# A recommendation tower on one core: row numbers added in one Pool instruction, 416 embedding gathers written out in a row

## What is computed

```python
e = jnp.stack([tbl_0[ids[:, 0]], ..., tbl_25[ids[:, 25]]], axis=1)      # 2048 x 26 x 64
x = layer_norm(dense_t @ Wd.T, gd, bd)                                 # 2048 x 128
y = layer_norm(jnp.einsum('bnd,ed->bne', e, Ws), gs, bs)               # 64 -> 128 for each row
y = layer_norm(jnp.einsum('bne,pn->bep', y, Wsi), gsi, bsi)            # 26 features -> 32
T = jnp.concatenate([x[:, None, :], jnp.swapaxes(y, 1, 2)], axis=1)    # 33 vectors of 128
Z = jnp.einsum('bnd,bmd->bnm', T, T)                                   # their products
out = layer_norm(Z[:, TRIL_I, TRIL_J] @ Wl.T, gl, bl)                  # 384 of 512 are used
h = concatenate([out, dense]); relu layers 768 -> 512 -> 256; y = h @ W_top3
```

## Time and profile before

| | |
|---|---|
| median of 3 runs | 756.58 us (755.66 to 756.83) |
| span of the profiled execution, first to last instruction | 754.8 us |
| time of the profiled execution itself | not listed apart |
| PE busy, DVE busy, ACT busy | 568.3 us, 501.8 us, 333.4 us |
| Pool busy | 460.1 us in 628 instructions |
| data moved | 36.43 MB, mean 48 GB/s |

### The profile page before, as it was taken

The page is one execution under the profiler, slowest core; times in us unless marked ns, Lnnn a source line. Parts: engine busy times, 40 slices in busy tenths (PEclk is TensorE's granted clock), DMA queues, the critical chain, the costliest instruction groups (busy, mean ns, idle before and its releaser), DMA issues.

```text
span 754.8 us, 18142 instructions
## 1 busy us (share of the span) xinstructions
PE 568.3 (75%) x6783; PEld 439.8 (58%) x6783; DVE 501.8 (66%) x837; ACT 333.4 (44%) x791; POOL 460.1 (61%) x628
## 2 busy tenths in 40 slices
PE   3675767777878787878787886877788677778866
PEld 3443546656565665757564755666465566656555
DVE  3757677777767777777767676766767576766720
ACT  0325535454445545444544354434544353543522
POOL 5666666666666666666666666666666666666200
PEclk9779879999999999999999799999999899997999
DMA  8311121212121211112121211112121111212010
GB/s 299 121 22 20 21 69 20 69 21 68 20 69 20 67 25 50 37 20 70 21 69 22 68 21 53 37 21 70 20 69 20 51 39 20 70 22 67 11 49 0
DMA packets 27202, 36.43 MB, mean 48 GB/s; under 512 B 8917, under 2 KB 17775, under 8 KB 26607
## 3 DMA queue, kind: packets, MB, share of 16 engines
q0 software_dynamic: 13312, 13.66, 9.5%
q1 hardware_dynamic: 13808, 21.65, 8.3%
HBM read 26.09 MB, written 9.18 MB: 47 GB/s over the span
## 4 chain that ended last, share of the span: by engine, by line
POOL 47%; issue 42%; PE 5%; DMA 2%; POOLq 1%; DVE 1%; ACT 1%; SPq 0%; DVEq 0%; ACTq 0%
POOL rows L549 40%; POOL ids L545 7%; PE bank_d L690 1%; PE bank_z L670 1%; DMA zx<-zs 1%; POOLq L547 1%; PE bank_a L634 1%; PE bank_z L701 1%; POOLq L548 0%; DMA rows<-in_table,ids 0%; PE bank_z L623 0%; DMA row_base<-in_row_base 0%; DVE mixed L417 0%; SPq L520 0%; ACT mixed L818 0%
## 5 line engine op out<-in xcount | busy, mean ns | idle before, releaser
L549 POOL DMA_INDIRECT rows<-in_table,ids x416 | 407.8, 980 | 237.5 <-POOL ids L545 165.8
L417 DVE TENSOR_TENSOR mixed<-bank_a,mixed 64x512 fp32r<-64x512 f32 x128 | 88.1, 688 | 90.5 <-ACT mixed L818 87.0
L818 ACT CAST mixed<-bank_a 64x512 fp32r<-64x512 f32 x128 | 74.3, 581 | 132.9 <-PE bank_a L634 131.3
L634 PE MATMUL bank_a<-wsi_b,scaled 128*128 128x192 f32 (+3 forms) x512 | 89.6, 319 | 44.7 <-DVE scaled L407 44.7
L634 PEld LDWEIGHTS bank_a<-wsi_b,scaled 128*128 128x128 f32 x512 | 77.7, 194 | 75.6 <-DVE scaled L407 75.0
L623 PE MATMUL bank_z<-gram,rows_t 128*128 128x128 f32 x416 | 74.7, 328 | 50.0 <-ACT rows_t L801 49.9
L435 DVE TENSOR_REDUCE y_var<-y_sq 128x32 f32<-128x1024 f32 x64 | 78.1, 1220 | 44.5 <-ACT y_sq L787 44.5
L787 ACT ACTIVATE y_sq<-y 128x512 f32<-128x512 f32 x128 | 80.6, 630 | 60.6 <-DVE y L425 53.9
L623 PEld LDWEIGHTS bank_z<-gram,rows_t 128*128 128x128 f32 x416 | 62.5, 227 | 63.9 <-ACT rows_t L801 63.9
L450 DVE TENSOR_TENSOR r_vec<-y,y_r 128x512 f32<-128x512 f32 x128 | 88.2, 690 | 2.2
L670 PE MATMUL bank_z<-wl,zd 128*128 128x512 f32 x160 | 77.6, 615 | 3.2 <-DMA zd<-zx 3.2
(11 more groups left out here) (106 smaller groups left out, 744.0 us busy)
## 6 DMA issues: line engine op xcount, KB each, us to landing
zx<-zs SPq DMA_DIRECT2D x16, 560.0 KB, 3.2
rows<-in_table,ids POOLq DMA_INDIRECT x416, 2.5
dense_t<-in_dense_t SPq DMA_DIRECT2D x1, 2048.0 KB, 8.7
wl<-in_wl SPq DMA_DIRECT2D x1, 1280.0 KB, 13.2
w<-in_w SPq DMA_DIRECT2D x1, 1280.0 KB, 16.2
zd<-zx SPq DMA_DIRECT2D x16, 80.0 KB
wsi_b<-in_wsi_b SPq DMA_DIRECT2D x1, 1248.0 KB, 11.4
zd<-zx SPq DMA_DIRECT2D x16, 70.0 KB
```

The source lines that it names most:

```text
L417: v.tensor_tensor(mixed[other, k % 2, blk, :], bank_m[own, :], mixed[own, k % 2, blk, :].bitcast(F32), ALU.subtract).then_inc(mix_lo, 1)
L549: nc.gpsimd.indirect_dma_start(rows[par][:, c, D * blk:D * (blk + 1)], None, io["table"], bass.IndirectOffsetOnAxis(ap=ids[par][:, n:n + 1 ...
L634: mm = pe.matmul(bank_m[:, o:o + num * PROJ], scaled[:, c, :], wsi_b[:, w0:w0 + num, :], start=(n == 0), stop=(n == len(wins) - 1), skip_g ...
L818: nc.scalar.copy(mixed[own, k % 2, blk, :], bank_m[own, :]).then_inc(mix_hi, 1)
```

## The change

The row numbers of all 16 tiles are added by one Pool instruction, in place in `ids_all` (128 partitions, 416 columns, `row_base` repeated 16 times), and Pool waits for it once. The two `ids` buffers and the semaphore `ids_seen` go. The hardware loop goes: the 416 gathers are written out one after the other. The wait for free space is made once for each quarter: before the gathers of quarter k, from tile 2 on, Pool waits for `rows_scaled` to reach k-7, which means that quarter k-8, the same one two tiles back, is scaled. The waits for `gathered` on Pool go. The gathers themselves, their order and their semaphores stay.

```diff
-        ids = [sb(f"ids{i}", [P, 2 * CHUNKS], I32) for i in range(2)]
...
-        ids_seen = sem("ids_seen")
...
-        def over_tiles(eng, body):
...
         @block.gpsimd
         def _(pool):
             pool.wait_ge(s_ids, 32)
-
-            def gather(t, par, more, load, inter, top):
-                if not load:
-                    return
-                if top:
-
-                    pool.wait_ge(rows_scaled, len(GROUPS) * (t - 1))
-
-                if top:
-                    for g in range(len(GROUPS)):
-                        pool.wait_ge(gathered[par][g], (t - par) * (16 * len(GROUPS[g])))
-                for n in range(2 * CHUNKS):
-                    c, blk = divmod(n, 2)
-                    if blk == 0:
-                        nc.gpsimd.tensor_tensor(ids[par][:, n:n + 2], ids_all[:, bass.ds(t * (2 * CHUNKS) + n, 2)],
-                                                row_base[:, n:n + 2], ALU.add).then_inc(ids_ready, 1)
-                        pool.wait_ge(ids_ready, t * CHUNKS + c + 1)
-                        pool.sem_inc(ids_seen, 1)
-                    nc.gpsimd.indirect_dma_start(
-                        rows[par][:, c, D * blk:D * (blk + 1)], None, io["table"],
-                        bass.IndirectOffsetOnAxis(ap=ids[par][:, n:n + 1], axis=0)).then_inc(gathered[par][group_of(c)], 16)
-
-            over_tiles(pool, gather)
+            nc.gpsimd.tensor_tensor(ids_all[:].rearrange("p (t n) -> p t n", t=TILES),
+                                    ids_all[:].rearrange("p (t n) -> p t n", t=TILES),
+                                    row_base[:].rearrange("p (o n) -> p o n", o=1).broadcast_to([P, TILES, 2 * CHUNKS]),
+                                    ALU.add).then_inc(ids_ready, 1)
+            pool.wait_ge(ids_ready, 1)
+
+            def gather(k):
+                t, q = divmod(k, BANKS)
+                if t >= 2:
+                    pool.wait_ge(rows_scaled, k - 2 * BANKS + 1)
+                for c in GROUPS[q]:
+                    for blk in range(2):
+                        n = t * 2 * CHUNKS + 2 * c + blk
+                        nc.gpsimd.indirect_dma_start(
+                            rows[t % 2][:, c, D * blk:D * (blk + 1)], None, io["table"],
+                            bass.IndirectOffsetOnAxis(ap=ids_all[:, n:n + 1], axis=0)).then_inc(gathered[t % 2][q], 16)
+
+            for k in range(QUARTERS):
+                gather(k)
```

## The result

The changed kernel takes **739.75 us** (median of 4 runs, 738.62 to 741.26), the kernel before 756.12 us: a ratio of **0.977, interval 0.975 to 0.980**. The forecast was 734.1 us in a range of 730 to 741. The direction and the mechanism hold; the gain is 16.4 us where 22.5 was forecast. The profiled execution took 740.86 us, with a span of 739.1 us (before: 754.8).

A forecast was written before the change was run, and what follows sets the result against it. Pool's gather sequence was taken to bound the kernel from about 371 us, the stages before; eight tiles at 40.7 us and three quarters start the last quarter 22.5 us earlier, tail unchanged: 756.6 - 22.5 = 734.1 us, range 730 to 741.

The forecast's parts named there:

- rival B: TensorE's clock stays at 0.94 as in the gather-bound stretch: 41.35 us a tile, gain 16.8, 739.8 us; chance 0.08.
- What bounds the kernel: Pool's sequence, 43.7 us a tile, binds from 371.97 us on; before that the stages pace themselves at 40.6.
- The spacing of the gathers: On Pool, without additions, waits and loop, gathers start 1.26 us apart: 32.8 us a tile.
- The threshold of 1.56 us: Any gather spacing on Pool below 40.6/26 = 1.56 us gives the same time, as the stages then set the pace.
- the addition and the wait for it: Between gather pairs on Pool: 0.20 + 0.81 us, to go from the rhythm of 3.23 us a chunk.
- The one big addition: Before Pool's first gather: about 1 us, that gather starting at 5.5 us; 15 us of cover, so no cost.
- The wait for each quarter: On Pool before a quarter's gathers: met at most quarters, 62 us of cover, costs nothing.
- The sum: From tile 7's start at 40.7 us a tile, the last quarter starts at 686.0, 22.5 us earlier: 734.1 us.
- the stages' own time: The chain from TensorE to ACT to DVE and back: 40.7 us a tile, 40.3 at full clock, 41.0 at 0.96.
- the tail: Behind the start of the last quarter on TensorE: 46.31 us, taken to stay.
- C: Gathers on Pool don't get faster, pace staying at 1.62 to 1.68 us each: 750 to 757 us; chance 0.05.
- D: Denser Pool gathers make DVE wait on SBUF, 61 us over 64 quarters: 795 us; chance 0.03 with the slow addition.

The follow-up runs named there:

- run 2: The changed kernel with the addition back in front of each chunk and Pool waiting for it, without the increment of `ids_seen`: 739.65 us, ratio 0.979.
- run 5: run 3 with the increment of `ids_seen` moved from behind the wait to the front of the addition: 739.92 us, ratio 0.980.
- run 3: run 2 with the increment of `ids_seen` behind the wait again, as the kernel before had it: 758.41 us, ratio 1.004.
- run 4: The changed kernel with one increment of `ids_seen` in front of each chunk's two gathers, no addition and no wait for one: 741.03 us, ratio 0.980.
- run 1: The changed kernel with Pool waiting for free space once a tile, not once a quarter: 739.42 us, ratio 0.979.
- run 7: The changed kernel with 3, 4, 0 and 2 extra matmuls in stages q = 0 to 3, before the product that waits for ACT: 729.14 us, ratio 0.965.
- run 9: run 7 with more extra matmuls: before the first transpose and first projection, before `mix` in stages q = 0 and 2, and in the tail: 722.26 us, ratio 0.956.
- run 8: The kernel before with the same extra matmuls as run 7: 753.09 us, ratio 0.996.
- run 6: The changed kernel with the gathers of the first two tiles alone, later tiles working on repeated rows: 740.38 us, ratio 0.980.

## Why the prediction was right, and what it missed

*The number.* The forecast's own range, from tiles of 40.3 us to tiles of 41.0, was 730.6 to 736.7 us, and 739.75 lies outside it. The stated range of 730 to 741 holds it because rival B's time was taken in. So the mechanism was forecast, and that the number is inside is in part luck.

*What bounds the kernel.* Right. The order was: the chain points to Pool, the quarters' starts say from when on Pool matters (371 us), and the stretch before gives the next limit. Tiles of 40.3 to 41.05 us came as read, but for one of 42.3. One reading was thin: 43.7 us a tile over the whole run, against 42.0 from the rhythm, was put down to long gathers alone, but the additions have a mean of 0.25 us (52.2 us in 208, the longest 2.49) instead of 0.20, which is 11 of the 28 us.

*The spacing of the gathers.* Forecast 1.26 us, measured 1.25. The threshold of 1.56 us fits as well: 1.35 us a gather (runs 2 and 5) gave the same time as 1.25, and 1.62 (run 3) didn't. But the step priced "the addition and the wait for it" as one block of 0.20 + 0.81 us. The addition and its wait are 0.20 us of what goes (2.70 against 2.50 a chunk), the increment, to which the prediction gave no cost, is 0.54. The sum was right and its label wrong: the one big addition, which names the change, wasn't needed for the gain.

*The one big addition.* Forecast about 1 us, measured 0.98; the estimate of 0.9 us from the Trainium skill's figure was near. The first gather starts at 4.74 us instead of the forecast 5.5: the forecast had kept the old gap of 0.95 us behind the addition, and 0.28 is left. With the increment in it (run 4) the gap is 0.94 again.

*The wait for each quarter.* Forecast to cost nothing, and so it did. It gives nothing either (run 1). The last gather starts at 622.3 us, where about 618 was forecast.

*The sum.* This is the term that was mis-sized: **the stages' own time**. The span fell by 15.7 us, not by 22.5. Between quarters 8 and 63 the gain is 20.1 us (581.60 to 561.53), inside the forecast's 19.9 to 26.0. The missing 6.8 us, from the windows: quarter 8 starts at 128.92 instead of 126.89, 2.0 us, in a stretch that I had taken as unchanged; from there to quarter 63 it is 561.5 us instead of the forecast 559.1, 2.4 us (tiles 7 to 14 take 328.84 us, 3.2 more than the eight of 40.7 that were forecast); the tail, also taken as unchanged, is 2.3 us longer. No instruction differs in any of these on TensorE, ACT or DVE. What differs is the granted clock: 0.89 against 0.96 in the tail, and 0.64 against 0.77 in the first tile, before (first line) and after:

```profile
33.20:83.12 49.92, 34.87 (x297) 21.64 (x298) 29.61 (x49) 19.23 (x41) 32.58 (x46) 0.77 0.11 21
```

```profile
33.10:85.79 52.69, 38.98 (x298) 25.29 (x299) 29.41 (x49) 19.18 (x41) 39.88 (x43) 0.64 0.12 27
```

That low clock is the cost is shown by runs 7 and 9. Why the changed kernel got more of it in the start and the tail is not. In the start it can be the luck of the profiled execution: seven traces without filling reach quarter 8 anywhere from 124.87 to 129.36 us, and the 126.89 of the kernel before lies among them. In the tail it comes back in each trace: 47.5 to 48.7 us at 0.89 to 0.93 in all eight with the gathers written out (run 9 apart), 46.31 and 45.28 us at 0.96 in the two of the old form (the kernel before and run 8). Run 3 has Pool's old pace and the long tail, so the pace isn't what makes it. The cause is open.

*Rivals.* B, the lower clock, was priced at 739.8 us with a chance of 0.08, and that is where the time came out, in part by luck. Its mechanism is half right: the tiles 7 to 14 kept a clock of 0.96, though the waits for rows had gone; but B took 0.94 and 41.35 us a tile, where 0.96 and 41.1 came; it had the whole miss in the tiles, and two thirds of it lay before and behind them. I tied the low clock to the waits for rows, and the filling runs show that TensorE's other gaps matter too. C fell with the spacing of 1.25 us, D with run 6.

## What to carry to other kernels

When an engine's chain is "instruction, idle until it is done, next instruction", look at what control instructions stand behind the wait: an increment cost 0.54 us there and nothing ahead of the addition. Before pricing a gain, read the next limit from a stretch where the first one doesn't bind. And where TensorE waits in short gaps and its granted clock is below 1.00, useless matmuls in the gaps, into a bank about to be overwritten, can pay: 10 us for one such place in each stage, 17 us with the start and the tail.

## What the runs showed of the hardware

- A semaphore increment as an instruction of its own on Pool: 0.54 us between a wait just met and a gather (gap 0.81 against 0.27 us), nothing measurable ahead of an addition or between gathers.
- The low clock came once in each tile from tile 6 to 13 of the changed kernel, where tiles 2 to 5 had been free of it with the same work: tiles 6 to 12 take 41.0 us each, and tile 13 42.3 at a mean clock of 0.92; tile 14 is free of it again. It shows first at the same place of a tile, in the product behind a wait of 1.48 us for ACT (1.65 us instead of 0.94), and the same wait stands in the free tiles. The first line below is of tile 7, the second of tile 3. In runs 2 and 4 every third tile from tile 5 on takes 42.3 us and the others 40.3, which adds up to the same 123 us for three. The filling ends it (runs 7 and 9); what picks the tile was not tried.

```profile
343.84 1.65 PE L599 MATMUL bank_z<-gram,rows_t 128*128 128x128 f32 x6 [1.48 <-ACT rows_t L777]
```

```profile
181.87 0.94 PE L599 MATMUL bank_z<-gram,rows_t 128*128 128x128 f32 x6 [1.48 <-ACT rows_t L777]
```

The window of tile 13:

```profile
577.47:619.77 42.30, 33.90 (x418) 27.32 (x417) 29.82 (x50) 19.69 (x46) 25.34 (x26) 0.92 0.16 43
```

- 416 gathers of 128 rows beside a busy DVE take nothing from it that can be measured: 740.4 us without 364 of them, 739.8 with all.
